# Two stretches of an order written out by hand: the opening, and the two attention stages, of a gated cross-attention kernel

## The reference

```python
x = x + tanh(g_xattn[0]) * L0_xattn(ctx, layernorm(x), ...)   # 32 half-heads of 8, differential softmax
x = x + tanh(g_ffn[0])   * L0_ffn(layernorm(x), ...)          # routed: 3 of 8 zones per batch row, gelu
x = x + tanh(g_xattn[1]) * L1_xattn(layernorm(x), ctx, ...)   # 16 heads of 16, then Wo
x = x + tanh(g_ffn[1])   * L1_ffn(layernorm(x), ...)          # silu(gate) * up, int32 weights / 127
```

## Time and profile before

| | us |
|---|---|
| median of three runs | 694.24 |
| the profiled execution, its own time | 694.52 |
| its span (first to last instruction) | 692.5 |
| TensorE busy | 627.4 (91%) |
| VectorE, ScalarE, GpSimd busy | 369.4, 370.3, 138.0 |
| mean granted TensorE clock | 0.954 of 2.4 GHz |

### The profile page before, as it was taken

How to read it: one execution, slowest core, us unless ns; L and a number is a source line. 1 busy time by engine, 2 the same in 40 slices (tenths; PEclk the granted TensorE clock), 3 DMA queues, 4 the chain that set the end, 5 groups by cost and what they waited for, 6 DMA issues and landing times.

```text
span 692.5 us, 10248 instructions
## 1 busy us (share of the span) xinstructions
PE 627.4 (91%) x3676; PEld 479.1 (69%) x3676; DVE 369.4 (53%) x817; ACT 370.3 (53%) x631; POOL 138.0 (20%) x206
## 2 busy tenths in 40 slices
PE   2698988988799999999999999999889789999996
PEld 2574555544378788888888777787567667888885
DVE  6677667767573523425546435434477655343332
ACT  4326747565865845646557435545756564243232
POOL 8433264243640000000000000001245212000000
PEclk9869999999999999999999999999988799999999
DMA  7321120112022030110303340000253000000000
GB/s 223 99 72 26 32 60 9 47 49 94 2 58 96 0 122 0 57 66 0 123 16 77 80 134 2 1 1 2 59 171 94 2 3 1 1 30 1 31 31 30
DMA packets 21969, 34.66 MB, mean 50 GB/s; under 512 B 4640, under 2 KB 13216, under 8 KB 21920
## 3 DMA queue, kind: packets, MB, share of 16 engines
q1 hardware_dynamic: 19648, 30.51, 14.3%
q0 software_dynamic: 1984, 3.44, 2.1%
q10 hardware_dynamic: 288, 0.07, 0.1%
HBM read 18.93 MB, written 2.10 MB: 30 GB/s over the span
## 4 chain that ended last, share of the span: by engine, by line
PE 77%; DVE 10%; ACT 5%; issue 4%; POOL 4%; DVEq 0%; ACTq 0%; POOLq 0%
PE SC L1157 28%; PE PV L1157 26%; PE AUX L1157 5%; PE PV L1175 5%; PE SC L1290 4%; PE AUX L1262 4%; DVE NM L1041 2%; ACT XN L752 2%; PE AUX L1218 2%; DVE O L1049 2%; DVE ST L959 1%; PE PV L1262 1%; POOL RSTD L626 1%; POOL QG L655 1%; PE AUX L1340 1%
## 5 line engine op out<-in xcount | busy, mean ns | idle before, releaser
L901 DVE TENSOR_TENSOR HL<-HF,HH 128x512 fp32r<-128x512 f32 x120 | 83.6, 696 | 155.9 <-ACT HH L847 155.6
L805 ACT ACTIVATE PB<-SC 77x1024 f32<-77x1024 f32 x96 | 94.2, 1014 | 45.2 <-PE SC L1290 45.0
L847 ACT ACTIVATE HH<-PV 128x512 fp32r<-128x512 f32 x96 | 57.3, 596 | 66.9 <-PE SC L1157 66.8
L842 ACT ACTIVATE HF<-PV 128x512 f32<-128x512 f32 x96 | 57.3, 597 | 57.0 <-PE PV L1157 54.9
L626 POOL TENSOR_TENSOR RSTD<-RSTD,NHALF 128x4 f32<-128x4 f32 x16 | 17.8, 1112 | 325.5 <-DVE RSTD L972 325.4
L1157 PE MATMUL PV<-XH,WAH 128*128 128x512 f32 x192 | 78.1, 407 | 1.1 <-DVE O L1049 1.1
L1157 PE MATMUL PV<-XL,WAH 128*128 128x512 f32 x192 | 76.4, 398 | 0.0
L1157 PE MATMUL PV<-XH,WAL 128*128 128x512 f32 x192 | 76.3, 397 | 0.0
L1157 PE MATMUL SC<-HL,WBH 128*128 128x512 f32 x192 | 75.6, 394 | 0.0
L1157 PE MATMUL SC<-HH,WBH 128*128 128x512 f32 x192 | 75.4, 392 | 0.0
L1157 PE MATMUL SC<-HH,WBL 128*128 128x512 f32 x192 | 75.0, 391 | 0.0
(11 more groups left out here) (229 smaller groups left out, 1217.7 us busy)
## 6 DMA issues: line engine op xcount, KB each, us to landing
QG<-QH SPq DMA_DIRECT2D x96, 64.0 KB, 2.0
WSA<-in_wa SPq DMA_DIRECT2D x6, 1024.0 KB, 5.0
WSB<-in_wb SPq DMA_DIRECT2D x12, 512.0 KB, 6.6
QG<-QL SPq DMA_DIRECT2D x48, 64.0 KB, 2.0
X<-in_x SPq DMA_DIRECT2D x4, 512.0 KB, 6.4
QG<-QH POOLq DMA_DIRECT2D x32, 64.0 KB, 2.2
out_x<-X SPq DMA_DIRECT2D x4, 512.0 KB, 2.6
QG<-QL POOLq DMA_DIRECT2D x16, 64.0 KB, 2.1
```

What stands on the lines that cost most here:

```text
L805: act.activation(probs(n)[0:S, :, :], SC[0:S, n % 2, :, :], ACT.Exp, scale=SCALE[a]).then_inc(exp_done, 1)
L842: act.activation(HF[s % 2][:, :], PV[:, s % 2, :], ACT.Gelu_apprx_tanh)
L847: act.activation(HH[s % 2][:, :], PV[:, s % 2, :], ACT.Gelu_apprx_tanh).then_inc(act_done, 1)
L901: return dve.tensor_tensor(dst, raw, hi.bitcast(F32), ALU.subtract)
```

## The change

Only `plan()` is changed. No instruction is added or removed; every function and every tile is as before, and all line numbers behind the function are four lower.

```diff
     steps = norm(ATT0, 0) + [("weights_split", 1), ("weights_split", 0), ("scale", ATT0, 0), ("turn", ATT0, 0)]
-    steps += keys(0, 0, 1) + [("query", 0, 0)] + moves(0, 0) + norm(ATT0, 1) + keys(0, 1, 3) + [("heads", 0, 0)]
+    steps += keys(0, 0, 1) + [("query", 0, 0)] + moves(0, 0) + keys(0, 1, 3) + [("heads", 0, 0)] + norm(ATT0, 1)
     first, second = maxima(0, 0, 0), maxima(0, 0, 1)
-    steps += [("scale", ATT0, 1)] + first[:6] + [("turn", ATT0, 1)] + first[6:] + [("coefficients",)] + keys(0, 3, 5)
-    steps += [("negmax", 0, 0, 0), ("query", 0, 1), ("q_move", 0, 1, 0)] + second[:10]
+    steps += first + [("scale", ATT0, 1), ("turn", ATT0, 1), ("negmax", 0, 0, 0), ("query", 0, 1), ("q_move", 0, 1, 0)]
+    steps += keys(0, 3, 5) + second[:8] + [("coefficients",)] + second[8:10]
     left = []
     for j in range(J):
         side = {}
-        last = (3, 5, 5, 4)[j]
+        last = (2, 4, 4, 3)[j]
         fillers = [(maxima(0, j, 1) if j else second[10:], 0, last)]
-        side.setdefault(last, []).append(("negmax", 0, j, 1))
+        side.setdefault(last + 1, []).append(("negmax", 0, j, 1))
         if j + 1 < J:
-            fillers.append((maxima(0, j + 1, 0), 6, 12))
+            fillers.append((maxima(0, j + 1, 0), 6, 11))
             side.setdefault(12, []).append(("negmax", 0, j + 1, 0))
...
         if j == 0:
             side.setdefault(0, []).extend(norm(ATT1, 3))
-            side.setdefault(5, []).extend([("ffn_load", 0), ("ffn_load", 1)])
-            side.setdefault(2, []).append(("scale", ATT1, 3))
-            side.setdefault(4, []).append(("turn", ATT1, 3))
-            side.setdefault(3, []).append(("q_move", 1, 2, 0))
-            side.setdefault(7, []).append(("q_move", 1, 2, 1))
+            side.setdefault(0, []).extend([("ffn_load", 0), ("ffn_load", 1)])
+            side.setdefault(3, []).extend([("scale", ATT1, 3), ("q_move", 1, 2, 0), ("ffn_split", 0, 0)])
+            side.setdefault(5, []).extend([("turn", ATT1, 3), ("ffn_split", 0, 1), ("ffn_load", 2)])
+            side.setdefault(7, []).extend([("q_move", 1, 2, 1), ("ffn_split", 1, 0)])
         if j == 1:
-            side.setdefault(1, []).append(("ffn_split", 0, 0))
-            side.setdefault(3, []).append(("ffn_split", 0, 1))
-            side.setdefault(4, []).append(("ffn_load", 2))
+            side.setdefault(2, []).append(("ffn_split", 1, 1))
             side.setdefault(5, []).append(("query", 1, 3))
-            side.setdefault(6, []).extend([("q_move", 1, 3, 0), ("ffn_split", 1, 0)])
-            side.setdefault(7, []).append(("ffn_split", 1, 1))
+            side.setdefault(6, []).append(("q_move", 1, 3, 0))
...
         if j == 2:
             side.setdefault(0, []).append(("q_move", 1, 3, 1))
-            side.setdefault(1, []).append(("ffn_split", 2, 0))
-            side.setdefault(3, []).append(("ffn_split", 2, 1))
...
         if j == 3:
             side.setdefault(0, []).append(("negmax", 1, 3, 1))
+            side.setdefault(2, []).append(("ffn_split", 2, 0))
+            side.setdefault(4, []).append(("ffn_split", 2, 1))
...
         if j > 1:
-            norm_in(side, 0, FFN1, j - 2, 1, 1)
+            norm_in(side, 0, FFN1, j - 2, 1, 3)
```

## The result

The changed kernel takes **702.5 us** in the median of 6 runs (699.0 to 705.6); the kernel before, in 6 runs beside it, 695.1 (692.2 to 704.6). The ratio is 1.011 with a 95% interval of 1.007 to 1.016: no change by the border of 2%, but slower beyond the measurement's uncertainty. The forecast of 681.5 has the wrong sign, and 702.5 lies outside its range.

A forecast was written before the change was run, and what follows sets the result against it. TensorE bounds the kernel, with waits and half-clock stretches in the opening and both attentions to recover. Gains 1.0 + 2.0 + 3.0 + 7.0 + 0 = 13.0 us from 694.5 gave 681.5, range 671.5 to 692.

The forecast's parts named there:

- the first attention's +2.0: First attention: denser maxima remove four 0.92 us waits ahead of `negmax`, half a microsecond counted for each; bounds 0 to 3.7.
- one short stretch of 3.4 us: Second attention, tiles 0 and 1: new holds near 503 to 507 risk 3.4 us at half clock, priced at 1.7.
- tile 3, put at 0: Second attention, tile 3: later turn, but XN about 1.7 us later; the 2.66 wait moves to unit 6; bounds -1.7 to +4.0.
- The third rival: First attention: mean clock falls from 0.93 to 0.84, costing 12.7 us, whole 696.2; decides from 0.85; chance 0.10.
- Three banks do not stretch: First attention: reductions sit closer, so TensorE meets the same VectorE one `max` earlier; hence half a microsecond per wait.
- Opening, forecast +1.0: Opening: key table and first maximum 1.0 us earlier, two waits covered, statistics and `coefficients` partly showing; bounds -1.7 to +2.6.
- Second attention, tiles 0 and 1, forecast +3.0: Tiles 0 and 1: 8.4 us from the 1.46 and 1.80 waits and half clock, less weight halves' holds and one short stretch.
- half clock for 10 us as now: Second attention, tiles 0 and 1: the lower bound's case, giving -2 (3.3 - 3.8 - 1.5).
- The rule on SBUF's two sides: VectorE and GpSimd lock one port pair; WG's second half takes up to 3.3 us, term 1.8 instead of 3.0, whole 682.7.
- Tile 2, forecast +7.0: Second attention, tile 2: 1.59 and 2.67 waits and the half-clock stretch go; replay 8.5 us; bounds 2.7 to 8.8.
- The clock falls at another place for 10 us: Failure sign, anywhere in the kernel: a new fall of the clock for 10 us, costing 5 us each time.
- The first attention moves by more than 4 us: Failure sign in the first attention: a move of over 4 us either way, its trade being the least replayable.

The follow-up runs named there:

- e2: Kernel before with only the first attention's denser maxima (both halves set closer); 699.7 us, ratio 1.007.
- e9: Kernel before with only the second attention's later scales and turns, e7's kernel run again; 689.1 us, ratio 0.988.
- e8: Kernel before with only the second halves of the first attention's maxima set closer; 697.3 us, ratio 1.003.
- e1: Kernel before with only the opening's new order; 694.9 us, ratio 0.999.
- e3: Kernel before with only the second attention's moves (later turns, weight loads and halves); 695.4 us, ratio 1.000.
- e4: Changed kernel with every max product of the first attention issued twice; 693.9 us, ratio to the kernel before 0.997.
- e6: e3's kernel with every max product of the first attention issued twice; 690.7 us, ratio to the kernel before 0.994.
- e10: Kernel before with weight loads and five weight halves placed as in the changed kernel, turns as before; 698.3 us, ratio 0.999.
- e7: Kernel before with only the second attention's later scales and turns, weight loads and halves unmoved; 683.3 us in 4 runs, ratio 0.983.
- e5: Kernel before with every max product of the first attention issued twice; 691.3 us, ratio 0.996.
- e12: e7's kernel with every max product of the first attention issued twice; 684.5 us, ratio to the kernel before 0.983.

## Why the prediction was wrong, point by point

**The step that failed is the first attention's +2.0**, "half a microsecond for each of the four waits": it put a fall of the clock at nothing, without a reason. The profile has -6.8 in its place, and e2, these maxima alone, 4.8 us by the medians. Behind it stands how the sum was built, "every term is a wait or a clock": each wait was priced at its own length, and the only loss of clock in the sum was one short stretch of 3.4 us in the second attention. That is the second step that failed: the stretch came and lasted 20.5. The third is tile 3, put at 0, which lost 2.8.

The third rival, "the denser first attention loses its clock", is what happened. It asked for a clock of 0.85 or less in 141.5 us and the profile has 0.85, though e9's profile, with the old order, has 0.83 in that window by chance. It had a chance of 0.10 and was priced at 696.2; the kernel took 702.5. Against it stood that "the total of waits shrinks". It did, but by 0.5 us (21.8 to 21.3), and the total says little about the clock: in e9, at half clock for 50.1 us, TensorE is idle for only 15.9. "Three banks do not stretch" was in the text of that very term, and should have been read as saying where the waits would go.

*Opening, forecast +1.0.* The mechanism was right: the key table wait is 3.67 instead of 4.42 us, the first maximum comes at 27.64 instead of 28.03 (though e2 and e8, with the old opening, have it at 27.09 and 27.12, so only the shorter wait can be read, 0.75 and not 1.0), behind three of them stands a wait of 1.19 for the statistics (I had said 1.2), the 0.91 is gone. `coefficients` shows as 1.37 at 50.88. At 49.4 the first exponential is 0.6 ahead; then come 6.8 us at half clock, and at unit 4 it is 2.6 behind. e1 has the term at about 0.

*First attention, forecast +2.0, bounds 0 to 3.7.* It is -6.8 in the profile and about -4 to -5 by e2's median: mis-sized and of the wrong sign, the largest single error. The four waits did go. What replaced them is longer: VectorE's own work among the reductions (the 1.33 ahead of 145.96) costs TensorE 1.73 where it cost 0.83, since no `values` lies under it now, and XN in tile 0 costs 2.13. The waits alone do not make the loss, since the idle time did not grow; the 25.6 us more at half clock (45.2 less 19.6) do, at 0.29 each 7.4 of the 10.0 us by which the stage is longer.

*Second attention, tiles 0 and 1, forecast +3.0, bounds -2 to 8.4.* -4, outside the bounds. 1.46 and 1.80 are gone, and there are waits for PB in tile 0 as said. Here they are, with the end of the stretch behind them:

```profile
514.56 0.70 PE L1286 MATMUL SC<-QG,KA 128*128 128x512 f32 x2 [0.94 <-ACT PB L801]
...
517.49 0.59 PE L1258 MATMUL AUX<-KA,QG 96*128 96x154 f32 x2 [1.13 <-DVE NM L1037]
518.01 1.91 PE L1171 MATMUL PV<-PB,V 77*17 77x128 f32 x32
...
533.01 0.77 PE L1153 MATMUL AUX<-XH,WQ1H 128*128 128x512 f32 x1
...
537.84 0.53 PE L1153 MATMUL PV<-XH,WQ1L 128*128 128x512 f32 x1
538.21 1.04 PE L1344 MATMUL AUX<-ident,MIX 128*128 128x128 f32 x8
```

I took their price to be at worst "half clock for 10 us as now", and in the sum 3.4. The stretch is 20.5 us, though no wait follows in it: the attention's products ran on at half speed until the last of the query's. In e3's profile, with the same waits, the stretch is 3.4 us long and the two tiles give +3.0, the term to the letter. So its waits were weighed rightly, and what it had wrong is the clock: in the other three profiles with these moves the stretch is 17.1 or 20.5 us and the tiles lose 2.3 to 3.8.

*The rule on SBUF's two sides.* GpSimd's add and VectorE's weight half met:

```profile
512.09 2.36 POOL L674 TENSOR_TENSOR X<-X,BOG 128x1024 f32<-128x1024 f32 x1 [1.60 <-DVE RZ L1051]
514.53 1.66 POOL L680 TENSOR_TENSOR MIX<-O,RZ 128x512 f32<-128x512 f32 x1
```

```profile
512.33 0.69 DVE L897 TENSOR_TENSOR XL<-AUX,XH 128x512 fp32r<-128x512 f32 x1 [0.33 <-ACT XH L740]
...
513.54 1.73 DVE L897 TENSOR_TENSOR WGL<-WI,WGH 128x768 fp32r<-128x768 int32 x1
```

The half (0.91 to 0.96 alone) takes 1.73: it ends 0.8 us after the add does (515.27 and 514.45), and the mix that starts behind it takes 1.66 instead of 1.07. The low half of XN, one of whose inputs lies in PSUM, takes its usual 0.69 beside the add. By the rule of the Trainium skill ("SBUF — State Buffer", "SBUF: two separate sides"), the half has the port only from the add's end, so it would end at 514.45 + 0.91 = 515.36: the trace agrees (515.27). It did not take the 3.3 that I had worked out, since it started when the add was 1.45 us old.

*Tile 2, forecast +7.0, replay 8.5.* 8.0, between unit 0 and unit 6. Units 4, 5 and 6 stand ahead of the turn, the 1.59 and 2.67 are gone, and so is the stretch at half clock:

```profile
556.84 0.63 PE L1344 MATMUL PV<-ident,MIX 128*128 128x128 f32 x4 [0.72 <-DVE NM L1037]
557.22 0.71 PE L1286 MATMUL SC<-QG,KA 128*128 128x512 f32 x2
...
558.33 0.63 PE L1214 MATMUL AUX<-ident,XN 128*128 128x128 f32 x4 [0.22 <-DVE XL L897]
```

Up to the start of tile 3 it is 6.7 of the 7.0 forecast, and the same 6.7 in e3, e4 and e6, whatever the clock did in tile 1. The turns alone give 3.2 and the halves alone 3.2 (e10), which is the forecast's own account: the 2.67 for the turn, and the 1.59 for the weight half ahead of the statistics, which is still there in e7's profile. This was the step worked out furthest, instruction by instruction, and it is the one that held.

*Tile 3, forecast 0, bounds -1.7 to +4.* The 2.66 moved to unit 6 as said, though it is 1.7 there, and the clock falls behind it for 6.8 us instead of 3.4. From unit 0 of the tile to the gated stage the lag grows from 7.8 to 10.6, which makes -2.8, below the bound:

```profile
575.56 1.08 PE L1286 MATMUL SC<-QG,KA 128*128 128x512 f32 x2 [1.68 <-ACT PB L801]
...
578.75 1.11 PE L1214 MATMUL AUX<-ident,XN 128*128 128x128 f32 x4 [1.26 <-DVE XL L897]
```

This was no chance: e3, e4 and e6 have -3.7 to -4.0, and with the turns alone it is +1.6 in all four profiles. The forecast had priced one half of the third weight, as a later XN. In the profile the first half costs 1.6 us by unit 4, where e7 loses nothing. From unit 6 to the gated stage the lag grows by 3.3, and by 1.2 in e7: the second half stands there, 0.96 us of VectorE at 576.18, ahead of the output and of the XL that the turn waits for.

*The clock's price.* "The clock falls at another place for 10 us (5 us each time)" named the right failure at too high a price: 0.29 us for each us at half clock, over all runs, not 0.5. The likely reason, which no run isolates, is that the other engines go on at their own speed and TensorE waits less for them: an exponential takes 1.01 us in the stretch at 576 and 1.00 ahead of it. "The first attention moves by more than 4 us" was the other condition, and it was met.

What stays open: why the clock falls where it does, and why one stretch at half clock ends after 3.4 us and another after 20.5 (TensorE never idle) or 34.1 (0.55 us idle). That gathered waits bring it down is argued from where it fell, and not shown. The clock also fell at 132.0 with no wait above 0.3 us in the 7 us ahead of it, so a wait is not always what precedes a fall. And whether the loss of the three parts is their sum was not told apart.

## What to carry to other kernels

Where an engine waits on a ring of few buffers, setting its steps closer may save next to nothing (0.5 us of 21.8 here): it moves the waits, and the granted clock that went with the new order cost more than the waits would have given. Before a sum is made of waits, ask for each one what the clock does where it goes to, and take the price of the clock from the spread of the kernel's own runs (here 4 us for each 0.01). Moving one long-latency consumer (the turn) behind work that is ready paid 1.2%; moving filler work (the weight halves) gave 3 us in the tile it left and took more than that where it went, in between steps that are each waited for.

## What the runs showed of the hardware

- Redundant products in TensorE's idle time paid: 128 more matmuls took the changed kernel from 702.5 to 693.9 us, and its mean clock from 0.936 to 0.966. In the kernel with the later turns they were worth 4.7 us. At equal clock they cost some 4 to 7 us by the table, an estimate (e4 against the changed kernel, e5, and e12 against e9), which is why the gain is smaller than the clock's part.
- The same instructions, behind the same waits, can run at full clock in one execution and at half clock for 34.1 us in another (e7 and e9, from 153.9 on). So can the stretch of 20.5 us in the second attention come out at 3.4 (the changed kernel and e3). One profile of such a kernel says little about a change of 1%.
- A VectorE subtraction of 128x768 with both inputs in SBUF took 1.73 us instead of 0.91 when it started in the midst of a GpSimd addition, and one of 128x512 with an input in PSUM took its usual 0.69 beside the same addition.
